# Late routing work of a gated attention and expert kernel: scatters ahead of the key rotation, gates in portions, gathers in three groups, the last batch stored by token tile

## The reference

```python
# x (4, 512, 256), ctx (4, 1024, 256), 16 heads of 64
lat, ctx = layer_norm(_layernorm(x)), layer_norm(context)
q = lat @ Wq;  k, v = split(ctx @ Wkv);  k = apply_rope(k, cos, sin)
attn = softmax(clip(q k^T / 8, -11, 11))
x = x + tanh(g_xattn) * ((attn v) @ Wo + bo)
...
logits = xf @ wr + br                      # xf (2048, 256), 4 experts
topk_vals, topk_idx = top_k(logits, 2);  gates = softmax(topk_vals)
y = gelu(xf @ w1[e] + b1[e]) @ w2[e] + b2[e]          # 256 -> 1024 -> 256
c = gelu(b1[e]) @ w2[e] + b2[e];  c_sum = c.sum(axis=0)
out = sum_k gates[k] * (y[idx_k] - c[idx_k] + c_sum)
x = x + tanh(g_ffn) * out
```

## Time and profile before

| | |
|---|---|
| median of 3 runs | 1193.79 us (1192.82 to 1195.61) |
| the profiled execution's own time | 1203.28 us |
| its span, first to last instruction | 1201.5 us |
| busy: PE, DVE, ACT, POOL | 93%, 85%, 54%, 51% |

### The profile page before, as it was taken

One profiled execution on the slowest core, in us unless ns is written; L12 is line 12 of the kernel. 1 busy time (PEld: TensorE's weight loads), 2 busy tenths in 40 slices (PEclk: granted clock), 3 DMA queues, 4 the chain that ended last, 5 costly groups with the idle time before them and its releaser, 6 DMA issues.

```text
span 1201.5 us, 22865 instructions
## 1 busy us (share of the span) xinstructions
PE 1123.1 (93%) x8087; PEld 758.0 (63%) x8087; DVE 1026.8 (85%) x1751; ACT 649.5 (54%) x1223; POOL 617.9 (51%) x593
## 2 busy tenths in 40 slices
PE   5799999999999999999999999997789989999987
PEld 3555555555555555465555556653379989999777
DVE  6699999898899998989999998889678777775886
ACT  4555566655456665455666455534456666663321
POOL 5333565343356535335644343238558767885750
PEclk9999999999999999999999999999999999999989
DMA  6000100000000000000000022002347555665102
GB/s 176 32 10 15 31 23 14 10 10 20 19 19 28 10 10 10 21 19 19 28 10 10 18 79 72 10 23 102 123 136 242 194 172 179 204 218 176 51 29 70
DMA packets 67080, 79.33 MB, mean 66 GB/s; under 512 B 10888, under 2 KB 60432, under 8 KB 66960
## 3 DMA queue, kind: packets, MB, share of 16 engines
q1 hardware_dynamic: 64640, 71.47, 18.5%
q0 software_dynamic: 2304, 6.29, 1.6%
q10 hardware_dynamic: 16, 0.00, 0.0%
HBM read 64.65 MB, written 13.11 MB: 65 GB/s over the span
## 4 chain that ended last, share of the span: by engine, by line
PE 68%; DVE 15%; POOL 6%; issue 6%; ACT 2%; DMA 1%; SPq 1%; another core or an unknown queue 0%; POOLq 0%; DVEq 0%; ACTq 0%
PE pv L1533 14%; PE sc L1519 12%; PE kv L1464 5%; PE kv L1466 4%; PE kv L1465 4%; PE sc L1464 4%; PE sc L1466 4%; PE sc L1465 4%; PE tr L1505 3%; DVE acc L1019 3%; PE mi L1464 3%; PE mi L1465 3%; PE mi L1466 3%; POOL slots_x L639 2%; PE mi L1543 2%
## 5 line engine op out<-in xcount | busy, mean ns | idle before, releaser
L800 ACT ACTIVATE prob<-sc 128x1024 f32<-128x1024 f32 x256 | 249.6, 1028 | 217.8 <-PE sc L1519 210.6
L610 POOL TENSOR_TENSOR rot_s<-k_raw,sinb 128x256 f32<-128x256 f32 x128 | 108.7, 850 | 389.3 <-ACT k_raw L748 389.3
L1533 PE MATMUL pv<-prob,val 128*32 128x512 f32 x2048 | 245.7, 597 | 3.0 <-DVE recip L1038 1.8
L1519 PE MATMUL sc<-q_hid,big 64*128 64x512 f32 x1536 | 214.7, 411 | 10.1 <-ACT prob L800 6.4
L1004 DVE TENSOR_SCALAR prob<-prob 128x1024 f32<-128x1024 f32 x256 | 183.8, 731 | 44.5 <-ACT prob L800 40.3
L1519 PEld LDWEIGHTS sc<-q_hid,big 64*128 64x128 f32 x1536 | 135.8, 186 | 115.0 <-issue 68.4
L1019 DVE TENSOR_TENSOR acc<-acc,prob 128x1024 f32<-128x1024 f32 x128 | 195.6, 1549 | 0.0
L614 POOL TENSOR_TENSOR rot_c<-rot_c,rot_s 128x256 f32<-128x256 f32 x128 | 122.0, 953 | 42.0 <-DVE rot_c L993 27.0
L1533 PEld LDWEIGHTS pv<-prob,val 128*32 128x32 f32 x2048 | 56.6, 109 | 111.9 <-issue 90.8
L1464 PE MATMUL kv<-big,acts 128*128 128x512 f32 x256 | 114.5, 447 | 6.2 <-DVE rot_c L993 5.0
L659 POOL TENSOR_TENSOR big<-prob,big 128x512 fp32r<-128x512 f32 x72 | 92.6, 1294 | 49.0 <-ACT big L827 45.2
(11 more groups left out here) (250 smaller groups left out, 2515.3 us busy)
## 6 DMA issues: line engine op xcount, KB each, us to landing
val<-in_L_ffn_w SPq DMA_DIRECT2D x18, 1024.0 KB, 5.6
prob<-in_L_ffn_w SPq DMA_DIRECT2D x18, 1024.0 KB, 5.6
rows<-in_ctx SPq DMA_DIRECT2D x32, 128.0 KB, 2.1
w_raw<-in_L_xattn_Wq SPq DMA_DIRECT2D x16, 256.0 KB, 2.6
w_raw<-in_L_xattn_Wo SPq DMA_DIRECT2D x64, 64.0 KB
slots_x<-c_aff SPq DMA_DIRECT2D x1, 3840.0 KB, 13.1
rows<-slots_x SPq DMA_DIRECT2D x15, 256.0 KB, 7.9
slots_y<-acc SPq DMA_DIRECT2D x15, 256.0 KB, 2.1
```

The costliest lines, as they stand in the source:

```text
L610: g.tensor_tensor(rot_s[:].rearrange("p (h a c) -> p h a c", h=4, a=2), kh[:, :, ::-1, :], sinb[:, t].unsqueeze(1).to_broadcast([P, 4, 2, ...
L800: a.activation(prob[:, s % 2, i, :], sc[i][:], ACT.Exp, scale=DH ** -0.5).then_inc(exp_done[i], 1)
L1519: last = mm(sc[i][:, h * N:(h + 1) * N], kst[rows_h, u % 2, j, lk, t * P:(t + 1) * P], q_sp[rows_h, p % 2, lq, :], start=lk + lq == 0, sto ...
L1533: last = mm(pv[g * 32:(g + 1) * 32, :], val[:, u % 2, 2 * c + i, at:at + 32], prob[:, s % 2, i, h * N:(h + 1) * N], start=c == 0 and i == ...
```

## The change

1. **Scatters.** In steps i = 20 to 23 two scatters stand ahead of the rotation, where three stood behind it. The other 16 come as 6, 6 and 4 at i = 24, 25 and 26 (before 4 and 8 at i = 24 and 25).
2. **Late gates.** `rank_gates` is cut into four portions, at m 1 and m 5 of jobs 6 and 7. ACT's exponential moves from job 7, m 0 to job 8, m 4. `last_gates` goes in two portions to job 9, m 0 and m 5, `b2_sum` in three to job 10, m 0, 4 and 6, `gelu_b1` to job 11, m 5.
3. **Gathers.** Eight each, between the chunks 3 and 4 of jobs 16, 17 and 18, in place of 12 after job 16 and 12 after job 17.
4. **Collects.** One tile at a time, at twelve places from m 4 of job 16 to m 2 of job 18.
5. **The constant.** In job 18 PE's `biases(3)` moves from m 3 to m 0 and DVE's part from m 5 to m 3; all four `finish` stand at m 4 to 7, ahead of the last `combine`, and the last batch is stored in four DMAs of one token tile (128 KB), each after its operation of the last `combine`. Before, `finish(3)` came after that `combine` and one DMA of 512 KB after it.

```diff
-            for t in range(NT):
+            for t in range(B - 1):
                 sp.wait_ge(fin, t + 1)
                 sp.dma_start(out[t].rearrange("(a p) d -> p a d", p=P), xacc[:, t * NT:(t + 1) * NT, :]).then_inc(stored, 16)
-            sp.wait_ge(stored, 16 * NT)
+            for i in range(NT):
+                sp.wait_ge(y_out, (E - 1) * NT + i + 1)
+                sp.dma_start(out[B - 1][i * P:(i + 1) * P, :], xacc[:, EARLY + i, :]).then_inc(stored, 16)
+            sp.wait_ge(stored, 16 * (B - 1 + NT))
...
                 make = not (last and u == UNITS - 1)
+                if last and R_RANK + 3 <= i < R_RANK + 7:
+                    for n in range(2):
+                        scatter((i - R_RANK - 3) * 2 + n)
                 if make:
                     rotate(*next_unit(b, u), s)
...
-                if last and R_RANK + 3 <= i < R_RANK + 7:
-                    for n in range(3):
-                        scatter((i - R_RANK - 3) * 3 + n)
-                if last and i == R_RANK + 7:
-                    for n in range(12, 16):
-                        scatter(n)
-                if last and i == R_RANK + 8:
-                    for n in range(16, 2 * EARLY):
+                if last and R_RANK + 7 <= i < R_RANK + 10:
+                    lo, hi = ((8, 14), (14, 20), (20, 24))[i - R_RANK - 7]
+                    for n in range(lo, hi):
                         scatter(n)
...
-                if SLOT_TILES < job < JOBS - 1:
-                    for n in range(EARLY):
-                        gather((job - SLOT_TILES - 1) * EARLY + n)
+                    if SLOT_TILES < job and chunk == 3:
+                        for n in range(8):
+                            gather((job - SLOT_TILES - 1) * 8 + n)
...
-                if job == LATE_TILE + 3 and m == 0:
+                if job == LATE_TILE + 4 and m == 4:
                     act.wait_ge(f_diff, 2)
...
-            def rank_gates(lo, hi):
+            def rank_gates(lo, hi, part=None):
...
-                for j in range(E):
+                for j in range(E) if part is None else range(part, part + 1):
...
             def combine(e):
 
                 dve.wait_ge(y_mm, (SLOT_TILES + e + 1) * MT)
+                if e == E - 1:
+                    dve.wait_ge(fin, B)
...
                 if t == B - 1:
-                    dve.wait_ge(y_out, E * NT)
+                    dve.wait_ge(y_out, (E - 1) * NT)
...
+            COLLECT = [4, 6, 7] + [MT + m for m in (0, 1, 3, 4, 6, 7)] + [2 * MT + m for m in (0, 1, 2)]
...
-                if job == LATE_TILE + 2 and m == 4:
-                    rank_gates(EARLY, B * NT)
-                if job == LATE_TILE + 3 and m == 4:
-                    last_gates(EARLY, B * NT)
-                if job == LATE_TILE + 4 and m == 4:
-                    b2_sum()
-                if job == LATE_TILE + 5 and m == 4:
+                if job in (LATE_TILE + 2, LATE_TILE + 3) and m in (1, 5):
+                    rank_gates(EARLY, B * NT, (job - LATE_TILE - 2) * 2 + m // 5)
+                if job == LATE_TILE + 5 and m in (0, 5):
+                    last_gates(EARLY, B * NT, m // 5)
+                if job == LATE_TILE + 6 and m in (0, 4, 6):
+                    b2_sum((0, 0, 0, 0, 2, 0, 3)[m])
+                if job == LATE_TILE + 7 and m == 5:
                     gelu_b1()
...
-                if e >= 0 and m == 5:
+                if 0 <= e < E - 1 and m == 5 or e == E - 1 and m == 3:
                     biases(e)
-                if e in (1, 2) and m in (3, 6, 7):
-                    j = (e - 1) * 6 + (0, 0, 0, 0, 0, 0, 2, 4)[m]
-                    collect(j)
-                    collect(j + 1)
-                if e == E - 1 and m in (5, 6, 7):
-                    finish(m - 5)
+                at = (e - 1) * MT + m
+                if at in COLLECT:
+                    collect(COLLECT.index(at))
+                if e == E - 1 and m in (4, 5, 6):
+                    finish(m - 4)
+                if e == E - 1 and m == 7:
+                    finish(B - 1)
             combine(E - 1)
-            finish(B - 1)
...
-                if job >= SLOT_TILES and m == 3:
+                if SLOT_TILES <= job < JOBS - 1 and m == 3 or job == JOBS - 1 and m == 0:
                     biases(job - SLOT_TILES)
```

More of the change, by code:

```diff
@@ L1242, in chain @@
                 dve.wait_ge(f_chain, n_chain[0])
-            def rank_gates(lo, hi):
+            def rank_gates(lo, hi, part=None):
                 R = hi - lo
                 lg, rank, more = f_logit[:, lo:hi, :], f_rank[:, lo:hi, :], f_tmp[:, lo:hi, :]
-                dve.wait_ge(f_lout, hi // 2)
-                if lo == 0:
-                    dve.wait_ge(l_tr, 2 * B)
-                chain(v.tensor_reduce(f_max[:, lo:hi], lg, mybir.AxisListType.X, ALU.max))
-                for j in range(E):
+                if part in (None, 0):
+                    dve.wait_ge(f_lout, hi // 2)
+                    if lo == 0:
+                        dve.wait_ge(l_tr, 2 * B)
+                    chain(v.tensor_reduce(f_max[:, lo:hi], lg, mybir.AxisListType.X, ALU.max))
+                for j in range(E) if part is None else range(part, part + 1):
                     to = rank if j == 0 else more
@@ L1262, in rank_gates, with last_gates @@
                     v.tensor_scalar(r_mask, rank, 2.0, None, ALU.is_lt).then_inc(r_masked, 1)
-                v.tensor_tensor(lg, lg, f_max[:, lo:hi].unsqueeze(2).to_broadcast([P, R, E]), ALU.subtract).then_inc(f_diff, 1)
-            def last_gates(lo, hi):
+                if part in (None, E - 1):
+                    v.tensor_tensor(lg, lg, f_max[:, lo:hi].unsqueeze(2).to_broadcast([P, R, E]), ALU.subtract).then_inc(f_diff, 1)
+            def last_gates(lo, hi, part=None):
                 R = hi - lo
-                dve.wait_ge(f_exp, 1 if lo == 0 else 2)
                 rank, gate = f_rank[:, lo:hi, :], f_gate[:, lo:hi, :]
-                chain(v.scalar_tensor_tensor(gate, rank, 2.0, f_tmp[:, lo:hi, :], ALU.is_lt, ALU.mult))
-                chain(v.tensor_reduce(f_sum[:, lo:hi], gate, mybir.AxisListType.X, ALU.add))
-                chain(v.reciprocal(f_inv[:, lo:hi], f_sum[:, lo:hi]))
-                chain(v.scalar_tensor_tensor(gate, gate, fgate, f_inv[:, lo:hi].unsqueeze(2).to_broadcast([P, R, E]),
-                                             ALU.mult, ALU.mult))
+                if part in (None, 0):
+                    dve.wait_ge(f_exp, 1 if lo == 0 else 2)
+                    chain(v.scalar_tensor_tensor(gate, rank, 2.0, f_tmp[:, lo:hi, :], ALU.is_lt, ALU.mult))
+                    chain(v.tensor_reduce(f_sum[:, lo:hi], gate, mybir.AxisListType.X, ALU.add))
+                if part in (None, 1):
+                    chain(v.reciprocal(f_inv[:, lo:hi], f_sum[:, lo:hi]))
+                    chain(v.scalar_tensor_tensor(gate, gate, fgate, f_inv[:, lo:hi].unsqueeze(2).to_broadcast([P, R, E]),
+                                                 ALU.mult, ALU.mult))
             def route_slots():
@@ L1336, in x_low, with b2_sum @@
                                 ALU.subtract).then_inc(f_xready, 1)
-            def b2_sum():
-                dve.wait_ge(ld_b2, 16)
-                dve.wait_ge(o_ready, B * PAIRS)
-                chain(v.tensor_tensor(csum, b2b[:, 0, :], b2b[:, 1, :], ALU.add))
-                for e in range(2, E):
+            def b2_sum(e):
+                if e == 0:
+                    dve.wait_ge(ld_b2, 16)
+                    dve.wait_ge(o_ready, B * PAIRS)
+                    chain(v.tensor_tensor(csum, b2b[:, 0, :], b2b[:, 1, :], ALU.add))
+                else:
                     chain(v.tensor_tensor(csum, csum, b2b[:, e, :], ALU.add))
```

## The result

The changed kernel takes 1188.58 us (median of 20 runs, 1184.02 to 1192.36), the kernel before 1193.12 (20 runs, 1186.93 to 1195.61). The ratio is 0.9964, with a 95% interval of 0.9950 to 0.9979: 4.3 us less (2.5 to 6.0), where I forecast 9.8 less. The time lies in the range; the gain is under half of the forecast one.

A forecast was written before the change was run, and what follows sets the result against it. PE was taken as the bound in the expert jobs, POOL's scatters in the last batch's attention. Scatters -2, late gates -7, gathers and collects +1.7 and the end -2.5 made -9.8: from 1193.8 to 1184 us, range 1177 to 1193.

The forecast's parts named there:

- Scatters: Last batch's attention: scatters start earlier, POOL stays busy, first piece 1.5 us earlier; -2 us, bounds -6.2 and 0.
- Late gates: Jobs 6 to 9: of 11.4 us lost, 4.5 stay after splitting the gates; -7 us, bounds -10.5 and -3.
- Over 1.9 us that leaves 0.6 for each of three portions: Rank portions: each meeting two chunks takes about 2.5 us, of which DVE's lead hides 1.9; 2.4 us in all.
- The exponential's term: ACT's moved exponential: two table loads and 0.2, 2.8 us, less 1.9, leave 0.9 us.
- The 1.2 us for `last_gates`: Its two portions in job 9 fall into POOL's chunk backlog and wait for chunk ends: 1.2 us added.
- Rival C: Gate portions cost nearly as much as the whole; late gates give 3 us: 1188 to 1191.4 us; chance 0.16.
- A: The forecast itself: 1180 to 1189 us; chance 0.54.
- Gathers and collects: Jobs 15 to 18: shorter stops save PE 2.5 us, the new wait before biases(3) costs 4.2; +1.7, bounds -9 and +8.
- The end: finish(3) leaves the path and the last store is 128 KB; -2.5 us, bounds -3.2 and -1.5.
- Rival B: PE's unexplained "issue" waits around the 12-gather runs go too, another 5 + 3.4 us: 1175.5 us; chance 0.14.
- D: POOL's chunk runs starve DVE at last_gates and before biases(3); slower, +5.8 us: 1199.6 us; chance 0.08.
- E: No change: scatters gain nothing, gates 3, the new wait eats the end's gain; 1191.5 to 1196 us; chance 0.08.

The follow-up runs named there:

- e1: The kernel before with only the scatters' part of the change (two apiece ahead of the rotation): 1196.20 us, ratio 1.0025.
- a1: The changed kernel measured again on another chip, in the third set: 1192.10 us, ratio to before 0.9876.
- f2: k3 with scatters two apiece, then 6, 6 and 4, behind the rotation: 1186.43 us, ratio to before 0.9950.
- s2: The kernel before with scatters two apiece, then 6, 6 and 4, behind the rotation as before: 1202.38 us, ratio 1.0044.
- e3: The kernel before with only gathers (8, 8, 8) and single collects changed, biases(3) left in place: 1195.70 us, ratio 1.0017.
- b1: The kernel before with only biases(3) moved, to m 0 on PE and m 3 on DVE: 1199.23 us, ratio 1.0028.
- n1: The changed kernel with the scatters put back as before: 1189.48 us, ratio to before 0.9852.
- e2: The kernel before with only the late gates split and moved: 1184.66 us, ratio 0.9926.
- e4: The kernel before with only the end changed (finishes ahead of the last combine, four stores): 1192.08 us, ratio 0.9991.
- s1: The kernel before with scatters three apiece moved ahead of the rotation, the rest 4 and 8: 1200.07 us, ratio 1.0019.
- g1: The kernel before with late gates and the end changed, finishes at m 5, 6, 7, 7: 1189.56 us, ratio 0.9946.
- g2: The same kernel as g1, run in the third set: 1197.70 us, ratio to before 0.9936.
- k2: g1 with the change's single collects in place of the pairs, gathers still 12 and 12: 1187.56 us, ratio to before 0.9965.
- k1: g1 with each group of 12 gathers behind its job's fourth chunk in place of the eighth: 1190.69 us, ratio to before 0.9987.
- n2: The changed kernel with scatters and biases(3) put back (late gates, gathers, collects and end stay): 1183.77 us, ratio to before 0.9823.
- k4: The same kernel as n2, run in the fourth set: 1185.56 us, ratio to before 0.9937.
- k3: n2 with gathers in six groups of four, behind chunks 2 and 6 of three jobs: 1180.64 us, ratio to before 0.9903.
- f1: k3 with scatters three apiece moved ahead of the rotation: 1179.60 us, ratio to before 0.9897.

## Why the prediction was off

**Scatters, the step that failed.** "Two scatters (3.1 us) cover the 2.3 us that ACT's next k_raw takes, so POOL doesn't go idle." POOL was idle for k_raw 3.7 us (2.6 in e1 and in a1), and what it did in the gaps it had to do later, ahead of the first piece. I compared the scatters with the k_raw of before, but in that profile the rotation came first: moved behind two scatters, it reaches PE later (3.27 us of wait), so the next k_raw leaves later too. The chain rotation, key turn, k_raw is a loop, and I had costed one side of it. The clock is the other thing that I left out. I had the first key turn "some 2 us later", on top of the 1.0 us that it waited before, and the trace of before has half clocks behind waits of PE of 3.80 us and 2.31 us (until 1002.42), yet the term has none. It came in all three profiles with two scatters ahead. In the profile after it accounts for all of the idle time, by size. In e1 it is shorter (PE's step from the first key turn to the second is 8.2 us, 1.5 over the 6.7 of before) and POOL is idle 2.6 us, so about 1 us is left to the loop without it. The term was -2 with bounds -6.2 and 0; it is +3.0 (1.0 to 5.0), outside them on the other side, and 5.0 of the 5.5 us by which I missed. I had the bound "0, if POOL gets gaps" and let it stop at nothing, with no reason that excluded a loss. Single long scatters are another part, as large as the idle time: 4.70, 4.70 and 4.69 us in e1, after and a1 and 5.02 in f2, some 3.4 over the mean of 1.26, where the longest with three apiece is 2.0. The sum held nothing for one. With the late start (0.8 us), the idle time (3.7) and the long scatter (3.4), less 2.3 for shorter rotations and other scatters, the 48.5 us of the forecast become the 54.1 of the profile after. No kernel has two scatters ahead and no long one, so how the +3.0 us divide between the two stays open. What makes them long is open too: they stand beside the loads of the first weights, but so do the scatters of before, and s2 had none.

**Late gates.** The mechanism was right, the size a little off: 8.8 us for 7 (6.1 to 11.6), with no half clock, and 2.7 us left in place of 4.5. The portions take DVE as long as I said, but PE waits only 1.6 us in all. "Over 1.9 us that leaves 0.6 for each of three portions", with 0.6 more for the one at m 1 of job 7, was a mis-sized term: one wait of PE stands behind a portion of the ranks, 0.5 us behind the fourth, so 0.5 for 2.4. The 1.2 us for `last_gates` was the other: no wait stands behind it. The exponential's term was right, 1.1 us for 0.9. Rival C, that portions cost nearly as much as the whole, is out, though the measured 1188.58 us lies in its range as well as in A's: the time came near C's because the scatters lost, not because the gates did.

**Gathers and collects, with biases(3).** +1.7 forecast; e3 gives +2.0 for the collects, and PE's wait ahead of `biases(3)` is 3.1 us where I had 3.3. b1 prices that part alone at +3.3 (0.1 to 6.7). So for the kernel as it runs in the first set the term should have been +3 to +5. The even chance of a half clock behind that wait was fair: it stands in a1 and n1 and not in the first measurement. The forecast took the four-chunk stop and the new wait rightly, but credited the removal of a wait of 2.5 us that typical executions don't have: in e2, with the same code there, that row has 0.4.

**The end.** -2.5 forecast; by the profiles of e4 (102.2 against 104.4) and of the change (4.1 against 6.3) -2.2, by e4's ratio -1.1 (-2.5 to +0.5). The profiles bear the size out; the ratio is smaller than the bound of -1.5 and not clear of zero.

**The sum** of the parts alone is -4.9, with b1's -1.6; the change measured -4.3. Each has an interval of 1.5 to 3.4 us either way, so the parts add up as well as can be told.

**Rival B**, the waits put down to issue, which I gave 0.14, isn't right or wrong but true of some sets and not of others (each ran on another chip): the changed kernel is at 0.9964 in one measurement and 0.9876 in the third set, where B's 1175.5 would be 0.985. In ten profiles with two groups of 12 gathers in the old place (before, e1, e2, e4, s1, s2, b1, g1, g2, k2) they stand in six, 1.3 to 5.4 us in pieces of 0.3 or more from 1075 us on, and k1, with 12 at the early place, has 1.2; in the nine profiles with groups of eight or four (after, e3, a1, n1, n2, k4, k3, f1, f2) in none. That the shorter groups remove them is shown as far as these go; what makes them is not: PE and ACT both start late there, and no row names what they wait for.

Rivals D and E didn't come. D's mechanism, DVE held by a whole run of chunks, did, in k1 and k2, at 6.8 and 5.9 us of PE.

## What to carry to other kernels

A queue that is the bound stays busy only if the work put ahead of the step that feeds a loop covers the whole loop as it will be then, not as it was; count how much later the step's own consumer, and so the next input, will come, and whether the consumer's longer wait costs it the clock as well. And look for every engine that waits for the moved work: two scatters behind the rotation made DVE wait for the eighth, which no part of the sum had. Backlogs are to be kept short: here DVE's operation lasted until the run of work that it met was over (10.93 us beside eight chunks, 6.60 beside four), so the length of the backlog sets the wait, and cutting the small operations up doesn't shorten it (k2). And before a long wait of one profile enters a sum, compare the profiled execution with the median: here it was 9.5 us over, and one stretch held more than all of it.

## What the runs showed of the hardware

- One DVE instruction of 128x256 with two SBUF inputs lasted 10.93 us beside eight back-to-back chunks of POOL (0.5 us otherwise). The Trainium skill ("SBUF — State Buffer", Who interferes with whom) has whoever starts first holding the ports for one instruction; here DVE didn't get them at any of the seven boundaries between POOL's chunks. By the profile DVE's instruction even started first, 0.7 us ahead of the first chunk and beside the last gather (1139.28 and 1139.99); why it wasn't done by then is open.
- The same kernel, before, had medians of 1192.8, 1197.6, 1206.8, 1192.1 and 1192.3 us in five sets, each on another chip, while one and the same kernel (n2 and k4) had 1183.8 and 1185.6 in the third and fourth: a ratio to a kernel with such waits differed by 1% between sets.
- Behind PE's wait of 3.3 us for the first rotation (after, e1, a1) or 4.5 us (s1, f1) the granted clock was half for 3.4 to 6.8 us; behind those of 1.0 to 1.6 us in the kernel before it stayed full. The length of the wait alone doesn't decide it: behind one and the same wait of 3.1 us ahead of `biases(3)` it was half in a1 and n1 and full in the first measurement.
- A scatter took POOL 0.97 to 2.0 us in fifteen profiles; in four of the five with two scatters apiece one of the 24 took 4.7 to 5.0 us.
